# The first layer's gated feed-forward of an audio tower, its fp32 products replaced by three rounded-format products each

## Chip, core and metric

The kernel runs on one core of a Trainium2 chip. The metric is the device time of one execution in microseconds (us), the median of several runs. Five engines work side by side, each through its own instructions in order: TensorE (PE in the rows, its weight loads PEld), VectorE (DVE), ScalarE (ACT), GpSimd (POOL) and SyncE (SP, which issues the DMAs). They wait for each other by semaphores.

## The reference, cut to what matters

The input is (64, 375, 256). A token layer halves the sequence (375 padded to 376, then 188 tokens) with a convolution and a layer norm. Two layers follow; each is an attention and a feed-forward with residuals. The change is in the first layer's feed-forward (width 704), whose operands are quantised to a 4-bit grid with one scale per 16 values:

```
h = tok(x)                                   # conv, mean of two, layer norm with gain and bias
h = h + attn0(layernorm(h))                  # 16 heads over 64 batch entries, softmax
def ffn0(x, w_gate, w_up, w_down):
    xq = fp4_quant_dequant(x)                # blocks of 16 along the last dimension
    g = xq @ fp4_quant_dequant(w_gate).T     # 256 -> 704
    u = xq @ fp4_quant_dequant(w_up).T       # 256 -> 704
    return fp4_quant_dequant(silu(g) * u) @ fp4_quant_dequant(w_down).T   # 704 -> 256
h = h + ffn0(layernorm(h), ...)
h = h + attn1(layernorm(h)); h = h + ffn1(h) # second layer, not touched
```

## The kernel before

**Stages.** `audio_tower` runs `layer0` (token layer and first layer) and then `layer1`. Each has a preparation block, in which weights are loaded and rebuilt, and a main block. All engines end the preparation block before one begins the main block. Between the layers the rows go through a scratch tensor in HBM.

**Preparation of layer0.** DVE quantises the three feed-forward weights, PE transposes them in 44 pieces through two PSUM banks, and ACT copies each piece into `gate_sb`, `up_sb` or `down_sb`.

**Main block of layer0.** The 64 x 188 tokens are worked on in 94 tiles of 128 rows (two token positions of all 64 entries; attention in the first layer runs over the batch entries of one position). The work is a software pipeline: in slot t the tile t goes through the convolution, norms and q, k, v; tile t-1 through scores, softmax and P times V; tile t-2 through the output projection, its norm and the quantisation of xq; tile t-3 through gate, up, tanh and the scales of hh; tile t-4 through hq, down and the store. `slots` unrolls 6 slots ahead of a loop over pairs of slots, and the last ones after it.

The order of each engine within a slot is written out by hand in its `slot` function (from L538 for PE, L616 for ACT, L781 for DVE, L836 for POOL). Nothing is reordered: an instruction that waits holds up all behind it on its engine. In short, for one slot:

- PE: conv, scores, transposes of att, gate and up of columns 0 to 351 (`gateup(t, 0)`), transposes of hq, output projection, `gateup(t, 1)`, `down`, transposes of ln1, transposes of P, q and k, v, P times V, transposes of xq.
- ACT: copy of v, of attT, of h1, tanh 0, exp, copy of hqT (640 and 64 columns), tanh 1, copies of ln1T and PT, magnitude of ln2, copy of q, magnitude of hh, eight copies of k, copy of xqT.
- DVE: division of att, conv result and its statistics, row maximum and shift of the scores, normalisation to h0, first half of hh, h1, statistics of h0 and h1, normalisation to ln1, moments of h1, normalisation to ln2, second half of hh, scales of ln2 and hh, h2, rounding of xq, rounding of hq.
- POOL: scaling of hq, rsqrt 0, h0 times gain, plus bias, rsqrt 1, rsqrt 2, h0b, scaling of hh, scaling of xq. Each rsqrt is an add (L832) and a power (L834) on one column.

**Products.** Gate and up (L468) are fp32: the transposed rows `xqT` (128 x 128, two blocks) are loaded as weights and 352 columns of the weight matrix stream by. Down (L497) takes six blocks of `hqT` and 256 columns of `down_sb`. In the trace an fp32 product is two MATMUL instructions.

**Rounded products.** The second layer already uses `product3` (L867). Each operand is held twice in the rounded format fp32r: a rounded high part, and a low part, which is the value minus the high part. Three matmuls are added up in PSUM: high by low, low by high, high by high.

```
def low(dst, src, hi, done):                 # as in layer1, on DVE there
    dve.tensor_tensor(dst, src, hi.bitcast(fp32), ALU.subtract).then_inc(S[done], 1)
```

Of the kernel before, what the change touches and what calls it, by code (L numbers as in the profile page):

```python
# [167 lines left out]
def layer0(nc, x, conv_w, conv_b, tok_g, tok_b, qkv_w, q_b, k_b, v_b, out_w, out_b, gate_w, up_w, down_w,  # L168
           h2_dram, ident, eps, exponent, w1, w1_loaded, wq, wk, wv, wo):
    with ExitStack() as ctx:  # L170
# [7 lines left out]
        conv_sb = sb("conv_sb", [128, 2 * KC, DM])  # L178
        q_sb, k_sb, v_sb = (sb(n, [128, KC, DM]) for n in ("q_sb", "k_sb", "v_sb"))
        outw_sb = sb("outw_sb", [128, KC, DM])  # L180
        gate_sb, up_sb = sb("gate_sb", [128, KC, F0]), sb("up_sb", [128, KC, F0])
        down_sb = sb("down_sb", [128, len(F0C), DM])
        convb_bc, tokg_bc, tokb_bc, outb_bc = (sb(n, [128, DM]) for n in ("convb_bc", "tokg_bc", "tokb_bc", "outb_bc"))
        qb_col, kb_col, vb_col = (sb(n, [128, KC]) for n in ("qb_col", "kb_col", "vb_col"))
        vb_wide = sb("vb_wide", [128, KC, 128])
# [18 lines left out]
        h1b = [sb(f"h1b{i}", [128, DM]) for i in range(2)]  # L204
        ln2 = sb("ln2", [128, DM])
        xq = sb("xq", [128, DM])
        xqT = sb("xqT", [128, KC, 128])
        tanh_g = sb("tanh_g", [128, GW])
        hh = sb("hh", [128, F0])
        hq = sb("hq", [128, F0])  # L210
        hqT = sb("hqT", [128, len(F0C), 128])
        h2 = [sb(f"h2_{i}", [128, DM]) for i in range(2)]
        binade = sb("binade", [128, 2048])
        small = sb("small", [128, 3, 128])
# [10 lines left out]
        wload, wconst, vones, wfold, vbias = (sem(n) for n in ("wload", "wconst", "vones", "wfold", "vbias"))  # L225
        wgate_loaded, wup_loaded, wdown_loaded = sem("wgate_loaded"), sem("wup_loaded"), sem("wdown_loaded")
        wquant, wtrans, wcopied = sem("wquant"), sem("wtrans"), sem("wcopied")
        with ExitStack() as tmp:
            graw, uraw = (tmp.enter_context(nc.sbuf_tensor(n, [WROWS, F0 // WROWS, DM], fp32)) for n in ("graw", "uraw"))
            draw = tmp.enter_context(nc.sbuf_tensor("draw", [128, KC, F0], fp32))  # L230
            with nc.Block() as block:
                @block.sync
                def _(sp):
# [37 lines left out]
                @block.vector  # L271
                def _(dve):
                    dve.wait_ge(wconst, 6)

                    for v in vblk:
                        for e in range(2):
                            for n in range(2):
                                c = e * (D0 + 1) + D0
                                dve.memset(v[64 * e:64 * e + 64, :, n, c:c + 1], 1.0).then_inc(vones, 1)

                    dve.wait_ge(wload, 16 * 12)
                    dve.wait_ge(wconst, 9)
# [49 lines left out]
                @block.scalar  # L332
                def _(act):
                    for n, (_, dst, rows, cols) in enumerate(JOBS):
                        act.wait_ge(wtrans, n + 1)
                        act.activation(dst, WBANK[n % 2][0:cols, 0:rows], ACT.Copy).then_inc(wcopied, 1)

# [7 lines left out]
            "xq_transposed", "xqT_copied", "gateup_done", "tanh_done", "hh_step", "hqa_step", "hv_ready", "habs_ready", "hqb_step",  # L345
            "hq_ready", "hq_transposed", "hqT_copied", "down_done", "h2_ready", "h2_stored0", "h2_stored1")}

        QK, YS, H1S, ST1, HH, SHIFT, ATT = KC + 4 * KC, 3, 3, 2, 4, 2, 2
        XM = 1 + SCALE_OPS + 1
# [38 lines left out]
        with nc.Block() as block:  # L388
# [25 lines left out]
            def _(pe):  # L414
# [24 lines left out]

                def xq_transpose(t):  # L440
                    bank_free(pe, t, [("ln1T_copied", t, 1, 1)],
                              [("attT_copied", t - 2, 1, 1), ("xqT_copied", t - 3, 1, 1)])
# [15 lines left out]
                def gateup(t, r):  # L458
                    z = t - 3
                    if r == 0:  # L460
                        bank_free(pe, t, [("qk_copied", t - 1, QK, QK), ("vblk_ready", t - 1, 4, 4)],
                                  [("hh_step", t - 4, HH, HH)])
                        wait(pe, "xqT_copied", z + 1)
                    else:
                        wait_step(pe, "hh_step", z, HH, 2)
                    for b, w in ((0, gate_sb), (1, up_sb)):
                        for c in range(KC):
                            last = pe.matmul(gu[:, b, 0:GW], xqT[:, c, :], w[:, c, r * GW:(r + 1) * GW],  # L468
                                             start=c == 0, stop=c == KC - 1)
                    last.then_inc(S["gateup_done"], 1)  # L470

                def att_transpose(t):
                    bank_free(pe, t, [("xqT_copied", t - 3, 1, 1)],
                              [("ln1T_copied", t - 1, 1, 1), ("attT_copied", t - 3, 1, 1)])
                    wait(pe, "att_step", t - 1, ATT)
                    av = att[:].rearrange("p h d -> p (h d)")
                    transposes(tp, [(128 * c, av[:, 128 * c:128 * (c + 1)]) for c in range(KC)], "att_transposed")

                def hq_transpose(t):
                    bank_free(pe, t, [("PT_copied", t - 2, 1, 1)], [("hqT_copied", t - 5, 2, 2)])  # L480
# [11 lines left out]

                def down(t):
                    bank_free(pe, t, [("h1_step", t - 2, H1S, 1)], [("y_step", t, YS, 1), ("h2_ready", t - 5, 1, 1)])
                    wait(pe, "hqT_copied", t - 3, 2)
                    for f, (o, w) in enumerate(F0C):
                        last = pe.matmul(cv[:, 0:DM], hqT[0:w, f, :], down_sb[0:w, f, :], start=f == 0,  # L497
                                         stop=f == len(F0C) - 1)
                    last.then_inc(S["down_done"], 1)

                def ln1_transpose(t):
                    bank_free(pe, t, [("attT_copied", t - 2, 1, 1)],
                              [("xqT_copied", t - 3, 1, 1), ("ln1T_copied", t - 1, 1, 1)])
                    wait(pe, "ln1_ready", t + 1)
                    transposes(tp, [(128 * c, ln1[:, 128 * c:128 * (c + 1)]) for c in range(KC)], "ln1_transposed")

                def p_transpose(t):
                    bank_free(pe, t, [("hqT_copied", t - 4, 2, 2)], [("PT_copied", t - 2, 1, 1)])
                    wait(pe, "probs_ready", t)
                    for i in range(PAIRS):  # L510
                        last = pe.transpose(pt[:, i // 4, 128 * (i % 4):128 * (i % 4 + 1)],
# [53 lines left out]
                        xq_transpose(t)  # L565

                pe.wait_ge(wfold, 6 + 2 * KC)
                pe.wait_ge(wcopied, len(JOBS))
                slots(pe, slot)

            @block.scalar
            def _(act):
# [43 lines left out]
                def slot(t, par):  # L616
# [12 lines left out]
                    if exists(t, 4):  # L629
                        wait(act, "hq_transposed", t - 3)  # L630
                        wait(act, "down_done", t - 4)
                        copy(hqT[:, 0:5, :], pt[:].rearrange("p a b -> p (a b)")[:, 0:640], "hqT_copied")
                        copy(hqT[0:64, 5, :], pt[0:64, 1, 128:256], "hqT_copied")
                    if exists(t, 3):
                        tanh(t - 3, 1)
                    if exists(t, 0):
# [192 lines left out]
            def _(pool):  # L829
                def rsqrt(t, k):  # L830
# [780 lines left out]
```

## Time and profile before

| | |
|---|---|
| median of 3 runs | 5284.75 us (5284.54 to 5287.21) |
| the profiled execution | 5283.22 us, its span 5281.1 us |
| PE busy | 4961.1 us, 94% of the span, 37144 instructions |
| DVE | 3369.7 us, 64% |
| ACT | 2636.0 us, 50% |
| POOL | 1866.8 us, 35% |
| granted TensorE clock, mean | 0.983 of 2.4 GHz |

The profile is of one execution. "Busy" is the union of an engine's instructions, without its waits; the share is of the whole span. The first layer lies from about 74 to 1923 us and the second behind it to the end; they have different limits, so the shares of the whole say little of one stage. In a row of the timeline, "x4" stands for four instructions merged, and the bracket gives the idle time of that engine just before and what ended it.

### The profile page before, as it was taken

The numbers are of one execution on the slowest core, as the hardware profiler recorded it, in microseconds if no ns is written. First come the engines' busy times: TensorE is split into PE (matmuls) and PEld (weight loads), VectorE is DVE, ScalarE is ACT, GpSimd is POOL, SyncE is SP. The second block draws the span as 40 slices with busy tenths as digits, with TensorE's granted clock in tenths as the row PEclk, the third lists the DMA queues.
The fourth block names the chain that finished last, engine by engine and source line by source line (L and its number), as shares of the span: only waits on it lengthen the run. The fifth ranks groups of instructions, "written<-read, shape, count | busy, mean of one in ns | idle before, by whom it ended". The sixth has DMA issues, their size and how long they took to land.

```text
span 5281.1 us, 108766 instructions
## 1 busy us (share of the span) xinstructions
PE 4961.1 (94%) x37144; PEld 4273.4 (81%) x37144; DVE 3369.7 (64%) x7355; ACT 2636.0 (50%) x5824; POOL 1866.8 (35%) x2017
## 2 busy tenths in 40 slices
PE   3999999999999949999999999999999999999997
PEld 2777777777777738998898989989988988989996
DVE  4888888888888843555555555555555555556555
ACT  2555555555555524555545554554554555555553
POOL 1444444444444412323333333333333334233333
PEclk9999999999999979999999999999999999999998
DMA  2000000000000010000000000000000000000000
GB/s 76 19 21 21 19 20 20 21 21 21 21 21 21 19 40 4 7 10 8 10 10 8 7 11 11 7 11 11 7 8 11 10 8 11 10 8 10 10 4 10
DMA packets 64990, 79.53 MB, mean 15 GB/s; under 512 B 8759, under 2 KB 51127, under 8 KB 64439
## 3 DMA queue, kind: packets, MB, share of 16 engines
q1 hardware_dynamic: 64566, 74.07, 4.9%
q8 instruction: 244, 4.00, 0.3%
q14 instruction: 180, 1.47, 0.1%
HBM read 49.40 MB, written 24.64 MB: 14 GB/s over the span
## 4 chain that ended last, share of the span: by engine, by line
PE 61%; issue 1%; DVE 1%; POOL 0%; ACT 0%; DMA 0%; SPq 0%; DVEq 0%; ACTq 0%; POOLq 0%
PE bA L869 10%; PE bA L870 8%; PE bA L871 8%; PE bO L1166 5%; PE bS L1145 4%; PE bO L1169 3%; PE bO L1172 3%; PE bA L1223 2%; PE bB L869 2%; PE bS L1146 2%; PE bS L1149 2%; PE bB L1136 2%; PE bB L1135 2%; PE bB L870 2%; PE bB L871 2%; PE bA L1224 2%
## 5 line engine op out<-in xcount | busy, mean ns | idle before, releaser
L1528 POOL TENSOR_TENSOR sqs_lo<-sq,sqs_hi 128x768 fp32r<-128x768 f32 x256 | 477.8, 1866 | 1065.7 <-ACT sqs_hi L1276 1058.4
L1370 DVE TENSOR_TENSOR qk_lo<-bA,qk_hi 128x384 fp32r<-128x384 f32 x512 | 284.4, 556 | 608.1 <-ACT qk_hi L1276 596.3
L1297 ACT ACTIVATE phiq<-bB 64x384 f32<-64x384 f32 x512 | 248.8, 486 | 792.5 <-PE bB L1136 786.2
L1520 POOL TENSOR_TENSOR yT_lo<-tanh_y,yT_hi 128x384 fp32r<-128x384 f32 x256 | 259.1, 1012 | 622.2 <-ACT yT_hi L1276 622.0
L1380 DVE TENSOR_TENSOR aT<-bS,mask 128x768 f32<-128x768 f32 x256 | 245.2, 958 | 158.7 <-PE bS L1149 158.7
L1166 PE MATMUL bO<-V,aT 128*128 128x65 f32 x2048 | 310.9, 274 | 0.0
L1145 PE MATMUL bS<-phiq,phik 128*128 128x256 f32 x1024 | 304.8, 379 | 0.0
L1328 ACT ACTIVATE pre<-bA,fc1b,fc1s 128x384 f32<-128x384 f32 x256 | 171.8, 671 | 251.3 <-PE bA L1224 251.3
L1166 PEld LDWEIGHTS bO<-V,aT 128*128 128x128 f32 x2048 | 275.3, 190 | 17.6 <-issue 0.2
L468 PE MATMUL gu<-gate_sb,xqT 128*128 128x352 f32 x752 | 266.9, 478 | 22.2 <-DVE hh L721 20.6
L1276 ACT ACTIVATE qk_hi<-bA 128x384 fp32r<-128x384 f32 x512 | 250.2, 489 | 64.0 <-PE bA L871 57.9
L497 PE MATMUL bank<-down_sb,hqT 128*128 128x256 f32 x1128 | 279.1, 389 | 1.0 <-ACT hqT L574 1.0
L1285 ACT ACTIVATE sq<-bA 128x384 f32<-128x384 f32 x512 | 251.5, 491 | 52.7 <-DVE qk_lo L1370 46.9
L614 ACT ACTIVATE tanh_g<-gu 128x352 f32<-128x352 f32 x188 | 87.3, 464 | 381.6 <-PE gu L468 381.6
L590 ACT ACTIVATE kblk<-gu,kb_masked,rowmask 128x128 f32<-128x128 f32 x752 | 271.5, 465 | 0.0
L109 POOL TENSOR_TENSOR hh<-hh,small 128x704 f32<-128x704 f32 x94 | 135.1, 1438 | 375.2 <-DVE small L103 375.2
L497 PEld LDWEIGHTS bank<-down_sb,hqT 128*128 128x128 f32 x1128 | 207.6, 190 | 72.3 <-issue 32.7
L468 PE MATMUL gu<-up_sb,xqT 128*128 128x352 f32 x752 | 255.7, 463 | 0.0
L869 PE MATMUL bA<-fc_lo,yT_hi 128*128 128x256 f32 x768 | 230.3, 300 | 10.7 <-POOL yT_lo L1520 5.6
L869 PE MATMUL bB<-qk_lo,omega_hi 128*128 128x384 f32 x512 | 186.4, 364 | 48.0 <-issue 42.9
L869 PE MATMUL bA<-wv_lo,xT_hi 128*128 128x256 f32 x768 | 228.6, 298 | 1.0 <-ACT sq L1285 1.0
L869 PE MATMUL bA<-wo_lo,attT_hi 128*128 128x256 f32 x768 | 225.9, 294 | 1.1 <-ACT pre L1328 1.1
(234 smaller groups left out, 15403.7 us busy)
## 6 DMA issues: line engine op xcount, KB each, us to landing
xT<-in_x SPq DMA_DIRECT2D x94, 256.0 KB, 2.7
h_scratch<-h SPq DMA_DIRECT2D x188, 64.0 KB, 1.9
hx<-h_scratch SPq DMA_DIRECT2D x32, 256.0 KB, 2.8
out<-res SPq DMA_DIRECT2D x32, 256.0 KB, 2.2
hx<-h_scratch SPq DMA_DIRECT2D x64, 64.0 KB, 2.5
out<-res SPq DMA_DIRECT2D x64, 60.0 KB, 1.8
q<-in_fc_q SPq DMA_DIRECT2D x2, 1024.0 KB, 6.2
wq_sb<-in_wq SPq DMA_DIRECT2D x1, 1024.0 KB, 5.0
```

Source lines behind the costliest of these rows:

```text
L468: last = pe.matmul(gu[:, b, 0:GW], xqT[:, c, :], w[:, c, r * GW:(r + 1) * GW], start=c == 0, stop=c == KC - 1)
L497: last = pe.matmul(cv[:, 0:DM], hqT[0:w, f, :], down_sb[0:w, f, :], start=f == 0, stop=f == len(F0C) - 1)
L590: act.activation(kblk[:, c, :, j, :], src, ACT.Identity, bias=kb_masked[:, c, j:j + 1], scale=rowmask[:, j:j + 1]).then_inc(S["qk_copied"], 1)
L869: pe.matmul(out, lhs[0], rhs[1], start=start, stop=False)
L870: pe.matmul(out, lhs[1], rhs[0], start=False, stop=False)
L871: return pe.matmul(out, lhs[0], rhs[0], start=False, stop=stop)
L1145: pe.matmul(o[:, :, 0:HEAD], keys, phiq[b][:, :, HEAD * i:HEAD * (i + 1)], start=True, stop=True)
L1166: pe.matmul(O[:, dst(i)], aT0[b][:, i, h, 0:HEAD], V[:, i, v], start=True, stop=True)
L1285: act.activation(sq[:, i, :], A[:, i, 0:NT], ACT.Square).then_inc(S["qk_hi"], 1)
L1370: dve.tensor_tensor(dst, src, hi.bitcast(fp32), ALU.subtract).then_inc(S[done], 1)
L1520: pool.tensor_tensor(yT[1][:, f % RING, :], tanh_y[f % 2][:], yT[0][:, f % RING, :].bitcast(fp32), ALU.subtract).then_inc(S["y_lo"], 1)
L1528: pool.tensor_tensor(sqs[1][:], sq[:], sqs[0][:].bitcast(fp32), ALU.subtract).then_inc(S["sq_lo"], 1)
```

## The change

The feed-forward weights are held as `gate_hi`, `gate_lo`, `up_hi`, `up_lo`, `down_hi`, `down_lo`; the full ones live in the preparation only. At its end ACT makes four rounded copies and DVE four subtractions. In the main block ACT copies each of xqT and hqT twice from PSUM, rounded and full, POOL subtracts one from the other, and gate, up and down are `product3`. New semaphores `xqT_split` and `hqT_split` say that the low parts are there; counts of the copies are doubled where PSUM banks are waited for.

```
# preparation
+ dve.wait_ge(whigh, n + 1)                                # four times: gate, up, down (5 blocks), down (last)
+ dve.tensor_tensor(lo, full, hi.bitcast(fp32), ALU.subtract).then_inc(wlow, 1)
+ act.wait_ge(wcopied, len(JOBS))
+ for hi, full in ((gate_hi, gate_sb), (up_hi, up_sb)):
+     act.activation(hi[:], full[:], ACT.Copy).then_inc(whigh, 1)
+ act.activation(down_hi[:, 0:5, :], down_sb[:, 0:5, :], ACT.Copy).then_inc(whigh, 1)
+ act.activation(down_hi[0:64, 5, :], down_sb[0:64, 5, :], ACT.Copy).then_inc(whigh, 1)
# PE, gateup
-         wait(pe, "xqT_copied", z + 1)
+         wait(pe, "xqT_split", z + 1)
-             last = pe.matmul(gu[:, b, 0:GW], xqT[:, c, :], w[:, c, r * GW:(r + 1) * GW], ...)
+             last = product3(pe, gu[:, b, 0:GW], (xqT_hi[:, c, :], xqT_lo[:, c, :]),
+                             (hi[:, c, cols], lo[:, c, cols]), c == 0, c == KC - 1)
# PE, down
-     wait(pe, "hqT_copied", t - 3, 2)
+     wait(pe, "hqT_split", t - 3, 2)
-         last = pe.matmul(cv[:, 0:DM], hqT[0:w, f, :], down_sb[0:w, f, :], ...)
+         last = product3(pe, cv[:, 0:DM], (hqT_hi[0:w, f, :], hqT_lo[0:w, f, :]),
+                         (down_hi[0:w, f, :], down_lo[0:w, f, :]), f == 0, f == len(F0C) - 1)
# PE, waits for banks: ("xqT_copied", t - 3, 1, 1) -> (.., 2, 2) and ("hqT_copied", .., 2, 2) -> (.., 4, 4)
# ACT, slot
      wait(act, "down_done", t - 4)
-     copy(hqT[:, 0:5, :], pt...[:, 0:640], "hqT_copied")
-     copy(hqT[0:64, 5, :], pt[0:64, 1, 128:256], "hqT_copied")
+     wait(act, "hqT_split", t - 4, 2)
+     for dst in (hqT_hi, hqT):
+         copy(dst[:, 0:5, :], pt...[:, 0:640], "hqT_copied")
+         copy(dst[0:64, 5, :], pt[0:64, 1, 128:256], "hqT_copied")
...
      wait(act, "gateup_done", t - 2, 2)
+     wait(act, "xqT_split", t - 2)
+     copy(xqT_hi[:], tp[:, 0:256], "xqT_copied")
      copy(xqT[:], tp[:, 0:256], "xqT_copied")
# POOL, slot
+ def low(dst, src, hi, done):
+     pool.tensor_tensor(dst, src, hi.bitcast(fp32), ALU.subtract).then_inc(S[done], 1)
          wait(pool, "st1", t + 1, ST1)
          rsqrt(t, 1)
+     if exists(t, 4):
+         wait(pool, "hqT_copied", t - 3, 4)
+         low(hqT_lo[:, 0:5, :], hqT[:, 0:5, :], hqT_hi[:, 0:5, :], "hqT_split")
+         low(hqT_lo[0:64, 5, :], hqT[0:64, 5, :], hqT_hi[0:64, 5, :], "hqT_split")
      if exists(t, 2):
          wait(pool, "h1_step", t - 1, H1S)
          rsqrt(t - 2, 2)
...
          fp4_scaled(pool, xq[:], xq[:], small_x, 1, 128, DM).then_inc(S["xq_ready"], 1)
+     if exists(t, 2):
+         wait(pool, "xqT_copied", t - 1, 2)
+         low(xqT_lo[:], xqT[:], xqT_hi[:], "xqT_split")
```

## Rows read from the trace of the kernel before

**Rows 1.** Busy time by stretch: us, each engine's busy time (instructions), PE clock, DMA.

```profile
1000.00:1500.00 500.00, 473.30 (x3704) 358.41 (x3700) 410.44 (x867) 271.38 (x692) 205.55 (x315) 1.00 0.08 21
```

**Rows 2.** One tile's instructions, 500 to 1500 us: ns min/median/max, first and last start.

```profile
L574 ACT ACTIVATE PT_sb<-pt x53: 1024/1024/1025, 503.0 to 1491.5; 128x1024 f32<-128x1024 f32 x53
```

**Rows 3.** Timeline of one slot: start, length, engine, line, operation, [idle before, releaser].

```profile
1003.51 0.42 ACT L574 ACTIVATE xqT<-bank 128x256 f32<-128x256 f32 x1
...
1005.23 1.35 PE L468 MATMUL gu<-gate_sb,xqT 128*128 128x352 f32 x4
...
1006.47 0.19 POOL L832 TENSOR_TENSOR rstd<-moments,eps 128x1 f32<-128x1 f32 x1 [1.85 <-DVE moments L672]
...
1007.60 0.82 PE L483 MATMUL pt<-ident,hq 128*128 128x128 f32 x6
...
1008.85 0.73 POOL L846 TENSOR_TENSOR h<-h,tokb_bc 128x256 f32<-128x256 f32 x1
...
1009.18 0.85 ACT L574 ACTIVATE hqT<-pt 128x640 f32<-128x640 f32 x2
...
1009.70 0.41 DVE L802 BATCH_NORM_STATS2 stats<-h 128x6 f32<-128x256 f32 x1
...
1010.80 0.55 POOL L834 TENSOR_TENSOR rstd<-rstd,exponent 128x1 f32<-128x1 f32 x1
1011.46 0.41 DVE L676 TENSOR_SCALAR ln<-h,moments,rstd 128x256 f32<-128x256 f32 x1 [0.65 <-POOL rstd L834]
...
1011.79 0.17 DVE L672 BATCH_NORM_AGGREGATE moments<-stats 128x2 f32<-128x6 f32 x1
1011.98 2.95 PE L497 MATMUL bank<-down_sb,hqT 128*128 128x256 f32 x12
1012.04 0.19 POOL L832 TENSOR_TENSOR rstd<-moments,eps 128x1 f32<-128x1 f32 x1 [0.69 <-DVE moments L672]
...
1012.90 0.81 DVE L676 TENSOR_SCALAR ln<-h,moments,rstd 128x256 f32<-128x256 f32 x1 [0.94 <-POOL rstd L834]
...
1014.85 0.44 PE L418 MATMUL bank<-ident,ln 128*128 128x128 f32 x2
...
1017.46 1.44 POOL L109 TENSOR_TENSOR hh<-hh,small 128x704 f32<-128x704 f32 x1 [3.90 <-DVE small L103]
...
1018.13 1.04 DVE L127 SCALAR_TENSOR_TENSOR ln<-binade_x,ln 128x256 f32<-128x256 f32 x1 [0.15 <-ACT binade_x L577]
...
1020.48 0.41 PE L418 MATMUL bank<-ident,xq 128*128 128x128 f32 x2 [0.55 <-POOL xq L109]
```

**Rows 4.** Groups of POOL's instructions in the second layer, 2400 to 5200 us.

```profile
L1528 POOL TENSOR_TENSOR sqs_lo<-sq,sqs_hi 128x768 fp32r<-128x768 f32 x219 | 409.5, 1870 | 862.9 <-ACT sqs_hi L1276 856.2
L1520 POOL TENSOR_TENSOR yT_lo<-tanh_y,yT_hi 128x384 fp32r<-128x384 f32 x221 | 223.8, 1013 | 517.3 <-ACT yT_hi L1276 517.1
```

**Rows 5.** Timeline of PE in the second layer: rounded products, 256 and 384 columns.

```profile
3003.48 0.28 PE L871 MATMUL bA<-wv_hi,xT_hi 128*128 128x256 f32 x1
...
3005.24 0.28 PE L871 MATMUL bA<-wv_hi,xT_hi 128*128 128x256 f32 x1
...
3011.35 0.34 PE L870 MATMUL bA<-xT_hi,wq_lo 128*128 128x384 f32 x1
...
3013.12 0.34 PE L871 MATMUL bA<-xT_hi,wk_hi 128*128 128x384 f32 x1
```

**Rows 6.** Busy time by stretch where PE had waited.

```profile
144.50:148.50 4.00, 2.30 (x21) 1.81 (x17) 3.78 (x6) 3.69 (x11) 1.43 (x3) 1.00 0.00 0
1974.70:1978.70 4.00, 1.32 (x9) 1.20 (x8) 0.42 (x1) 0.81 (x2) 1.80 (x1) 1.00 0.00 0
1979.00:1982.00 3.00, 3.00 (x11) 3.00 (x11) 0.00 (x0) 1.55 (x4) 0.00 (x0) 0.50 0.00 0
```

**Rows 7.** Timeline of the second layer's preparation: weight copy and subtraction.

```profile
1925.39 1.91 ACT L951 ACTIVATE wq_hi<-wq_sb 128x2048 fp32r<-128x2048 f32 x1 [8.70 <-PEq L388]
...
1939.61 2.29 DVE L967 TENSOR_TENSOR wq_lo<-wq_sb,wq_hi 128x2048 fp32r<-128x2048 f32 x1
```

More of the change, by code:

```diff
@@ L180, in layer0 @@
         outw_sb = sb("outw_sb", [128, KC, DM])
-        gate_sb, up_sb = sb("gate_sb", [128, KC, F0]), sb("up_sb", [128, KC, F0])
-        down_sb = sb("down_sb", [128, len(F0C), DM])
+        gate_hi, up_hi = sb("gate_hi", [128, KC, F0], fp32r), sb("up_hi", [128, KC, F0], fp32r)
+        gate_lo, up_lo = sb("gate_lo", [128, KC, F0], fp32r), sb("up_lo", [128, KC, F0], fp32r)
+        down_hi, down_lo = (sb(n, [128, len(F0C), DM], fp32r) for n in ("down_hi", "down_lo"))
         convb_bc, tokg_bc, tokb_bc, outb_bc = (sb(n, [128, DM]) for n in ("convb_bc", "tokg_bc", "tokb_bc", "outb_bc"))
@@ L206, in layer0 @@
         xq = sb("xq", [128, DM])
-        xqT = sb("xqT", [128, KC, 128])
+        xqT, xqT_hi, xqT_lo = (sb(n, [128, KC, 128], t) for n, t in (("xqT", fp32), ("xqT_hi", fp32r), ("xqT_lo", fp32r)))
         tanh_g = sb("tanh_g", [128, GW])
@@ L210, in layer0 @@
         hq = sb("hq", [128, F0])
-        hqT = sb("hqT", [128, len(F0C), 128])
+        hqT, hqT_hi, hqT_lo = (sb(n, [128, len(F0C), 128], t) for n, t in
+                               (("hqT", fp32), ("hqT_hi", fp32r), ("hqT_lo", fp32r)))
         h2 = [sb(f"h2_{i}", [128, DM]) for i in range(2)]
@@ L227, in layer0 @@
         wquant, wtrans, wcopied = sem("wquant"), sem("wtrans"), sem("wcopied")
+        whigh, wlow = sem("whigh"), sem("wlow")
         with ExitStack() as tmp:
@@ L230, in layer0 @@
             draw = tmp.enter_context(nc.sbuf_tensor("draw", [128, KC, F0], fp32))
+            gate_sb, up_sb, down_sb = (tmp.enter_context(nc.sbuf_tensor(n, s, fp32)) for n, s in (
+                ("gate_sb", [128, KC, F0]), ("up_sb", [128, KC, F0]), ("down_sb", [128, len(F0C), DM])))
             with nc.Block() as block:
@@ L306, in _ @@
                     st.end()
+                    for n, (lo, full, hi) in enumerate((
+                            (gate_lo[:], gate_sb[:], gate_hi[:]), (up_lo[:], up_sb[:], up_hi[:]),
+                            (down_lo[:, 0:5, :], down_sb[:, 0:5, :], down_hi[:, 0:5, :]),
+                            (down_lo[0:64, 5, :], down_sb[0:64, 5, :], down_hi[0:64, 5, :]))):
+                        dve.wait_ge(whigh, n + 1)
+                        dve.tensor_tensor(lo, full, hi.bitcast(fp32), ALU.subtract).then_inc(wlow, 1)
                 JOBS = [(raw, j, c, WROWS, 128, dst, c, j * WROWS) for raw, dst in ((graw, gate_sb), (uraw, up_sb))
@@ L344, in layer0 @@
             "att_transposed", "attT_copied", "outproj_done", "h1_step", "h1b_ready", "xq_step", "xabs_ready", "xq_ready",
-            "xq_transposed", "xqT_copied", "gateup_done", "tanh_done", "hh_step", "hqa_step", "hv_ready", "habs_ready", "hqb_step",
-            "hq_ready", "hq_transposed", "hqT_copied", "down_done", "h2_ready", "h2_stored0", "h2_stored1")}
+            "xq_transposed", "xqT_copied", "xqT_split", "gateup_done", "tanh_done", "hh_step", "hqa_step", "hv_ready", "habs_ready", "hqb_step",
+            "hq_ready", "hq_transposed", "hqT_copied", "hqT_split", "down_done", "h2_ready", "h2_stored0", "h2_stored1")}
         QK, YS, H1S, ST1, HH, SHIFT, ATT = KC + 4 * KC, 3, 3, 2, 4, 2, 2
@@ L441, in xq_transpose @@
                     bank_free(pe, t, [("ln1T_copied", t, 1, 1)],
-                              [("attT_copied", t - 2, 1, 1), ("xqT_copied", t - 3, 1, 1)])
+                              [("attT_copied", t - 2, 1, 1), ("xqT_copied", t - 3, 2, 2)])
                     wait(pe, "xq_ready", t - 1)
@@ L462, in gateup @@
                                   [("hh_step", t - 4, HH, HH)])
-                        wait(pe, "xqT_copied", z + 1)
+                        wait(pe, "xqT_split", z + 1)
                     else:
                         wait_step(pe, "hh_step", z, HH, 2)
-                    for b, w in ((0, gate_sb), (1, up_sb)):
+                    cols = slice(r * GW, (r + 1) * GW)
+                    for b, hi, lo in ((0, gate_hi, gate_lo), (1, up_hi, up_lo)):
                         for c in range(KC):
-                            last = pe.matmul(gu[:, b, 0:GW], xqT[:, c, :], w[:, c, r * GW:(r + 1) * GW],
-                                             start=c == 0, stop=c == KC - 1)
+                            last = product3(pe, gu[:, b, 0:GW], (xqT_hi[:, c, :], xqT_lo[:, c, :]),
+                                            (hi[:, c, cols], lo[:, c, cols]), c == 0, c == KC - 1)
                     last.then_inc(S["gateup_done"], 1)
                 def att_transpose(t):
-                    bank_free(pe, t, [("xqT_copied", t - 3, 1, 1)],
+                    bank_free(pe, t, [("xqT_copied", t - 3, 2, 2)],
                               [("ln1T_copied", t - 1, 1, 1), ("attT_copied", t - 3, 1, 1)])
@@ L479, in hq_transpose @@
                 def hq_transpose(t):
-                    bank_free(pe, t, [("PT_copied", t - 2, 1, 1)], [("hqT_copied", t - 5, 2, 2)])
+                    bank_free(pe, t, [("PT_copied", t - 2, 1, 1)], [("hqT_copied", t - 5, 4, 4)])
                     wait(pe, "hq_ready", t - 3)
@@ L494, in down @@
                     bank_free(pe, t, [("h1_step", t - 2, H1S, 1)], [("y_step", t, YS, 1), ("h2_ready", t - 5, 1, 1)])
-                    wait(pe, "hqT_copied", t - 3, 2)
+                    wait(pe, "hqT_split", t - 3, 2)
                     for f, (o, w) in enumerate(F0C):
-                        last = pe.matmul(cv[:, 0:DM], hqT[0:w, f, :], down_sb[0:w, f, :], start=f == 0,
-                                         stop=f == len(F0C) - 1)
+                        last = product3(pe, cv[:, 0:DM], (hqT_hi[0:w, f, :], hqT_lo[0:w, f, :]),
+                                        (down_hi[0:w, f, :], down_lo[0:w, f, :]), f == 0,
+                                        f == len(F0C) - 1)
                     last.then_inc(S["down_done"], 1)
@@ L502, in ln1_transpose @@
                     bank_free(pe, t, [("attT_copied", t - 2, 1, 1)],
-                              [("xqT_copied", t - 3, 1, 1), ("ln1T_copied", t - 1, 1, 1)])
+                              [("xqT_copied", t - 3, 2, 2), ("ln1T_copied", t - 1, 1, 1)])
                     wait(pe, "ln1_ready", t + 1)
@@ L507, in p_transpose @@
                 def p_transpose(t):
-                    bank_free(pe, t, [("hqT_copied", t - 4, 2, 2)], [("PT_copied", t - 2, 1, 1)])
+                    bank_free(pe, t, [("hqT_copied", t - 4, 4, 4)], [("PT_copied", t - 2, 1, 1)])
                     wait(pe, "probs_ready", t)
@@ L567, in _ @@
                 pe.wait_ge(wfold, 6 + 2 * KC)
-                pe.wait_ge(wcopied, len(JOBS))
+                pe.wait_ge(wlow, 4)
                 slots(pe, slot)
@@ L631, in slot @@
                         wait(act, "down_done", t - 4)
-                        copy(hqT[:, 0:5, :], pt[:].rearrange("p a b -> p (a b)")[:, 0:640], "hqT_copied")
-                        copy(hqT[0:64, 5, :], pt[0:64, 1, 128:256], "hqT_copied")
+                        wait(act, "hqT_split", t - 4, 2)
+                        for dst in (hqT_hi, hqT):
+                            copy(dst[:, 0:5, :], pt[:].rearrange("p a b -> p (a b)")[:, 0:640], "hqT_copied")
+                            copy(dst[0:64, 5, :], pt[0:64, 1, 128:256], "hqT_copied")
                     if exists(t, 3):
```

## Prediction

> **What bounds the kernel now.** I read the stretches first. In the first layer's steady part TensorE (PE) is busy 473.3 of 500 us at full clock [rows 1]: it looks like the bound, 94.7%. One slot (one of 94 tiles) takes (1491.5 - 503.0) / 52 = 19.01 us [rows 2], so PE works 18.0 us of it and waits 1.0. Then I read one slot in order of time and followed what ends PE's waits [rows 3]. Its last piece, the transposes of xq, waits 0.55 us for GpSimd (POOL), which got xq from VectorE (DVE). Going back from there, a chain closes on itself: PE conv and scores, DVE's row maximum and shift, its normalisation, POOL's two products for h0 (the second ends at 1009.58), DVE's statistics of h0 (1009.70), POOL's rsqrt 1 (ends 1011.35), DVE's normalisation of ln1 (1011.46) and moments of h1 (end 1011.96), POOL's rsqrt 2 (starts 1012.04), DVE's normalisation of ln2 (1012.90). From there DVE works on with one gap, of 0.15 us (1018.13), up to xq; POOL scales xq, PE transposes it (1020.48), and the next conv follows. So the period is that of this DVE/POOL chain. Of PE only the xq transposes, conv and scores are in it. Gate, up and down, which the change touches, lie beside it.
>
> **PE work removed.** An fp32 product is two instructions, a rounded one is one. Now: four gate products and four instructions of up of a half (1005.23 to 1007.60, [rows 3]) are 8 instructions in 2.37 us, 0.296 us each, so 0.59 us a product. Rounded products in the second layer: 15 instructions of 256 columns from 3003.48 to 3005.24 are 0.117 us each; 10 of 384 columns from 3011.35 to 3013.12 are 0.177 [rows 5]. For 352 columns I interpolate 0.162. A half becomes 12 x 0.162 = 1.94 us, 0.43 less; the second half the same. Down is 12 instructions in 2.87 us (1011.98 to 1014.85) and becomes 18 x 0.117 = 2.11, 0.76 less. PE does 0.43 + 0.43 + 0.76 = 1.6 us less a slot.
>
> What the chain gets of it: the first half ends 0.43 earlier, so tanh and the first DVE products of hh do too; but the statistics of h0 then wait for POOL's product that ends at 1009.58, so they start at about 1009.64 instead of 1009.70. Gain 0.06 us. rsqrt 1 ends at 1011.29.
>
> **The split of xq** (ACT one copy more, POOL one subtraction of 256). ACT copies xqT at 1003.51 in 0.42 us; with a second copy behind it both are done by 4.35 (times from here on are us after 1000, in this slot). POOL subtracts 256 elements. Two rows of POOL subtractions with rounded output give 1013 ns for 384 and 1870 ns for 768 [rows 4], that is 0.156 + 2.23 ns an element: 0.73 us, to 5.1. Behind it in POOL's queue stands the scaling of hq, 1.4 us (as the 128x704 scaling at 1017.46), so to 6.5, when DVE's work beside it is in PSUM; then rsqrt 0, issued at 6.47 before. The gate products started at 5.23, and the transposes of hq, which wait for the scaling, at 7.60 (7.2 now). Everything meets its time with up to 0.7 us to spare or none: I cost it at nothing. If ACT were 0.2 us later, rsqrt 0 would be late by about that, and the normalisation to h0 and the chain with it by no more than that: 0.2.
>
> **The split of hq** (ACT two copies more, POOL two subtractions, 640 and 64 elements). Both copies now take 0.85 us from 9.18 [rows 3]; ACT starts no later and does four, to 10.9 at most. POOL is in rsqrt 1 until 11.29 and, in program order, the two subtractions stand right after it and ahead of rsqrt 2. By the same two rows they cost 0.156 + 2.23 x 640 = 1.58 and 0.156 + 2.23 x 64 = 0.30, together 1.88 [rows 4]: POOL is free at 13.17. But DVE's normalisation of ln1 and the moments of h1 also stand before rsqrt 2. What DVE does beside a POOL instruction: the product of 256 at 1018.13 took 1.04 us and ended 0.27 us after POOL's scaling of hh (17.46 + 1.44 = 18.90) [rows 3], as if it only streamed once POOL was done. ln1's normalisation starts at 11.40, in the first subtraction (11.29 to 12.87), so it ends shortly after that, at about 13.0; the moments of h1, 0.17, are done when POOL is free. rsqrt 2 starts at about 13.25, where it started at 12.04: +1.2 us, with the gain of 0.06 already taken off. The Trainium skill, SBUF — State Buffer, section "SBUF: two separate sides", calls the port pair of VectorE and GpSimd an exclusive lock held for the whole instruction, the loser fully blocked; that row agrees (0.27 us after POOL's end). If the two shared the ports instead, ln1 would be done well before POOL is free, and the delay would be 13.17 - 12.04 = 1.13; the lock may add up to 0.3.
>
> Bounds: subtractions as cheap as POOL's scaling of hh (1.44 us for 704, [rows 3]; 1.57 for the two after a fixed part each) instead of 1.88: free at 12.86, +0.8 us. Above, with ln1 held back by both subtractions: 13.17 + 0.15 for its rest + 0.17 for the moments is 13.5, +1.45. I take 1.2 because the rows that give 1.88 are the same operation with the same output format.
>
> All that follows rsqrt 2 in the chain (h0b, ln2, the second half of hh, scales, xq, hq) is as now and has no slack: xq comes 1.2 us later, so do the next conv and scores. New period about 20.2 us.
>
> **The wait of down.** Down could start 0.86 earlier than its 11.98, at 11.1, and waits for the low part until 13.2: 2.1 us idle. Queued behind: ln1's transposes, P's, q, k, v, PV, xq's. From ln1's transposes (14.85) to the end of PV (20.48 less the 0.55 of waiting) PE takes 5.1 us. With down 2.1 long it ends PV at 13.2 + 2.1 + 5.1 = 20.4; xq's transposes are due at 20.48 + 1.2 = 21.7: hidden, with 1.2 us to spare, as long as the clock stays. The other new waits (ACT for the subtractions of the slot before, PE's bank waits for twice the count) are met a slot earlier.
>
> **Once.** The weight splits stand after the last weight copy and before the barrier; after it the loop's first loads start, and the first conv waits for them. ACT copies at 1.91 us for 2048 elements and DVE subtracts at 2.29 [rows 7]; first copy 1408: 1.33; then DVE 1.6, 1.6, 1.45, 0.4: together 6.4 us. DVE is nearly back to back, ACT's later copies are beside it. In the last slots nothing covers copies and subtraction ahead of the last down: +2.6, less about 1 for shorter down at low clock: +2.
>
> **Sum.** 92 slots x 1.2 = 110; + 6.4 + 2 = 118.4. The profiled execution took 5283.2 (span 5281.1 and 2.1 around it), 1.5 below the median of the runs. So 5401.6 in its terms, 5403 in the median's.
>
> **Rivals.**
> 1. *The clock falls.* Nothing in the steady part loses it now. It stayed at full after PE was busy 2.30 of 4 us; it fell to half (1.2 GHz) after 1.32 of 4, and stood at half for the next 3 us shown [rows 6]. The new gap leaves 1.9 of 4: between. 3 us at half cost PE 1.5, of which 1.2 are covered: +0.3 a slot where it happens, more where it stays longer. In every slot +28, at twice that price +55. Beside the 5403: 5410 to 5458. The Trainium skill, TensorE: Matmul & The Clock Gate, section "What's actually happening", says that the throttled state is the default and activity lifts it; the two rows agree in kind. By that rule alone the time would be this rival's. Chance 0.2.
> 2. *PE sets the period* (other side: faster). PE is busy 94.7% [rows 1]; if every us taken off PE shortened the slot, 1.6 x 94 = 150 less, 8 more for what comes once: 5143. It needs rsqrt 2 not to be delayed, so the subtractions would have to fit in the 0.69 us between rsqrt 1 and rsqrt 2. At 1.57 at least they don't. It decides from a delay of rsqrt 2 under 0.06 us, the gain found above. Against it: PE waits for xq at the end of the slot [rows 3], so PE is not the one that is late. For it: its share. 0.08.
> 3. *The subtractions are cheap*, as POOL's scalings are, so that rsqrt 2 is 0.8 to 0.9 late: 92 x 0.8 + 8.4 + 5284.7 = 5367, to 5376. Against it: both subtraction rows. 0.09.
> 4. Delay and gains cancel within measurement: 0.03; no mechanism in the rows gives it.
>
> **How the numbers follow.** Forecast 0.60, its own range 5376 to 5427 (0.9 to 1.45 us a slot). Rival 1 0.20, rival 3 0.09, rival 2 0.08, rival 4 0.03. The range to hold 8 in 10 goes from 5355 (rival 3 in) to 5450 (rival 1 in) and leaves out rivals 2 and 4 and tails. A change of over 0.2% (10.6 us) can be told from none: slower 0.89, same 0.03, faster 0.08.
>
> **What would show it.** The period between two copies of PT in the first layer: 20.2 us, PE busy 16.4 of it. rsqrt 2's POOL add 1.9 us after rsqrt 1's end instead of 0.69, released by DVE's moments or by POOL itself. Subtractions of 640 at 1.5 to 1.6 us. PE idle about 2 us before down, ended by POOL, and about 1 us before xq's transposes. ln1's normalisation near 1.5 us instead of 0.41. Granted clock 1.00 in the steady part. The first conv 6.4 us later. The second layer unchanged. I am wrong if rsqrt 2 is not later, if the period is under 19.5 (rival 2), or if the clock in the steady part is under 0.97 (rival 1).

## The result and the profile after

The changed kernel takes 5432.9 us (median of 4 runs, 5431.7 to 5433.3), the one before 5284.7: ratio 1.028, 95% interval 1.026 to 1.030. It is slower by 148 us. The profiled execution has a span of 5431.5 us.

First the same two views as [rows 1] and [rows 2]: busy time in 1000 to 1500 us, and the copies of PT in 500 to 1500 us.

```profile
1000.00:1500.00 500.00, 428.32 (x3730) 373.08 (x3729) 397.51 (x806) 271.68 (x703) 256.09 (x369) 0.96 0.07 19
```

```profile
L592 ACT ACTIVATE PT_sb<-pt x49: 1023/1024/1026, 499.6 to 1481.2; 128x1024 f32<-128x1024 f32 x49
```

The slot is (1481.2 - 499.6) / 48 = 20.45 us, 1.44 more than before. PE is busy 85.7% instead of 94.7%, and the granted clock is 0.96 instead of 1.00. Over the whole first layer the copies of PT run from 105.9 to 1871.9 before and from 112.7 to 2013.3 after: 134.6 us in the slots and 6.8 at the start; the layer's end adds 1.6. Of the 150.4 us between the spans, 143.0 lie in the first layer (up to the second layer's first weight copy, which starts at 1925.4 before and at 2068.4 after) and 7.4 in the second, whose code is the same.

One slot in order of time, as in [rows 3] (start, length, engine, line, operation, [idle before, releaser]):

```profile
1001.38 0.74 POOL L871 TENSOR_TENSOR h<-h,tokb_bc 128x256 f32<-128x256 f32 x1
...
1002.16 0.43 DVE L824 BATCH_NORM_STATS2 stats<-h 128x6 f32<-128x256 f32 x1 [0.29 <-POOL h L871]
...
1003.27 0.55 POOL L856 TENSOR_TENSOR rstd<-rstd,exponent 128x1 f32<-128x1 f32 x1
...
1003.79 1.99 POOL L859 TENSOR_TENSOR hqT_lo<-hqT,hqT_hi 128x640 fp32r<-128x640 f32 x2
...
1003.93 1.54 DVE L698 TENSOR_SCALAR ln<-h,moments,rstd 128x256 f32<-128x256 f32 x1 [0.65 <-POOL rstd L856]
1005.39 0.17 DVE L694 BATCH_NORM_AGGREGATE moments<-stats 128x2 f32<-128x6 f32 x1
1005.75 0.18 POOL L854 TENSOR_TENSOR rstd<-moments,eps 128x1 f32<-128x1 f32 x1
...
1005.93 0.37 PE L901 MATMUL bank<-down_lo,hqT_hi 128*128 128x256 f32 x1 [2.14 <-POOL hqT_lo L859]
...
1006.59 0.81 DVE L698 TENSOR_SCALAR ln<-h,moments,rstd 128x256 f32<-128x256 f32 x1 [1.03 <-POOL rstd L856]
...
1009.91 0.44 PE L434 MATMUL bank<-ident,ln 128*128 128x128 f32 x2
...
1012.62 0.43 DVE L127 SCALAR_TENSOR_TENSOR ln<-binade_x,ln 128x256 f32<-128x256 f32 x1 [0.94 <-ACT binade_x L595]
```

Rsqrt 1 ends at 1003.82 and rsqrt 2 starts at 1005.75: 1.93 us apart, where they were 0.69 apart [rows 3]. The two subtractions fill that gap. DVE's normalisation of ln1 takes 1.54 us instead of 0.41 and ends at 1005.47, 0.15 after the first subtraction. PE waits 2.14 us for the low part ahead of down.

Then down takes from 1005.93 to 1009.91, 3.98 us, where 2.1 was forecast. The busy time by stretch around it (columns as in [rows 1]):

```profile
1002.00:1006.00 4.00, 1.86 (x13) 1.60 (x11) 2.60 (x5) 1.32 (x4) 2.97 (x6) 1.00 0.00 0
1006.20:1009.50 3.30, 3.30 (x16) 3.08 (x15) 2.77 (x8) 0.00 (x0) 1.05 (x2) 0.50 0.00 0
```

After 4 us with 1.86 us of work the clock fell to 1.2 GHz for the whole of down. This does not happen in every slot. Three slots later the clock stayed at full after nearly the same stretch (its busy time, then that of down; below it PE's rows of the same slot):

```profile
1063.78:1067.78 4.00, 1.93 (x13) 1.67 (x12) 2.73 (x6) 1.47 (x5) 3.03 (x6) 1.00 0.00 0
1068.00:1070.00 2.00, 2.00 (x17) 1.87 (x17) 1.53 (x3) 0.00 (x0) 1.11 (x2) 1.00 0.00 0
```

```profile
1067.78 0.36 PE L901 MATMUL bank<-down_lo,hqT_hi 128*128 128x256 f32 x1 [2.07 <-POOL hqT_lo L859]
...
1070.26 0.44 PE L434 MATMUL bank<-ident,ln 128*128 128x128 f32 x2
...
1076.03 0.41 PE L434 MATMUL bank<-ident,xq 128*128 128x128 f32 x2 [0.69 <-POOL xq L109]
```

Here down takes 2.48 us (1067.78 to 1070.26), and PE later waits 0.69 us for xq. In the slot whose clock fell that wait is gone: PE's transposes of xq start at 1014.92 without one.

```profile
1014.92 0.44 PE L434 MATMUL bank<-ident,xq 128*128 128x128 f32 x2
```

So a fall makes down 1.5 us longer (3.98 instead of 2.48), the wait of 0.7 covers that much of it, and PE is in the chain for the rest, 0.8.

What decides which slots fall is not shown: the wait ahead of down was 2.04 to 2.14 us in the slots that fell and 2.07 to 2.10 in the others. The exp of ACT, once a slot, shows them (start and length, copied from 500 to 600 us):

```profile
509.61 1.05 ACT L646 ACTIVATE P<-P 128x1024 f32<-128x1024 f32 x1
529.78 1.05 ACT L646 ACTIVATE P<-P 128x1024 f32<-128x1024 f32 x1
549.72 1.05 ACT L646 ACTIVATE P<-P 128x1024 f32<-128x1024 f32 x1
570.63 1.05 ACT L646 ACTIVATE P<-P 128x1024 f32<-128x1024 f32 x1
591.47 1.05 ACT L646 ACTIVATE P<-P 128x1024 f32<-128x1024 f32 x1
```

Slots of 20.17 and 19.94 us alternate with slots of 20.91 and 20.84. The short pair averages 20.06, 1.05 above the 19.01 of before; the long ones cost 0.8 more, and about half of the slots are long. So the slot's 1.44 us are 1.05 from a delay in every slot and 0.39 from the clock.

### The profile page after: what moved, and what is told of

Read it like the earlier page. It is cut to its first block, busy times and chain, and to the rows that moved or that the text cites. A ratio compares the mean times of both kernels' runs of the same rounds, so it can differ in the third digit from the quotient of the medians.

```text
span 5431.5 us, 112180 instructions
## 1 busy us (share of the span) xinstructions
PE 4926.0 (91%) x38460; PEld 4437.6 (82%) x38460; DVE 3435.4 (63%) x7359; ACT 2727.1 (50%) x6110; POOL 2111.3 (39%) x2299
## 4 chain that ended last, share of the span: by engine, by line
PE 59%; issue 1%; DVE 0%; ACT 0%; POOL 0%; DMA 0%; SPq 0%; DVEq 0%; ACTq 0%; POOLq 0%
PE bA L901 10%; PE bA L902 8%; PE bA L903 8%; PE bO L1198 5%; PE bS L1177 4%; PE bO L1201 3%; PE bO L1204 2%; PE bA L1255 2%; PE bB L901 2%; PE bS L1178 2%; PE bS L1181 2%; PE bB L1168 2%; PE bB L1167 2%; PE bB L903 2%; PE bB L902 2%; PE bA L1256 2%
## 5 line engine op out<-in xcount | busy, mean ns | idle before, releaser
L901 PE MATMUL bank<-down_lo,hqT_hi 128*128 128x256 f32 x564 | 209.0, 371 | 194.8 <-POOL hqT_lo L859 194.8
L901 PEld LDWEIGHTS bank<-down_lo,hqT_hi 128*128 128x128 f32 x564 | 136.5, 242 | 235.4 <-DVE moments L694 211.4
L698 DVE TENSOR_SCALAR ln<-h,moments,rstd 128x256 f32<-128x256 f32 x188 | 217.1, 1155 | 161.3 <-POOL rstd L856 161.3
L592 ACT ACTIVATE ln1T<-bank 128x256 f32<-128x256 f32 x94 | 36.1, 384 | 497.5 <-PE bank L434 497.5
L1402 DVE TENSOR_TENSOR attT_lo<-bT,attT_hi 128x384 fp32r<-128x384 f32 x256 | 142.6, 557 | 129.3 <-ACT attT_hi L1308 129.1
```

Source lines behind the costliest of these rows:

```text
L901: pe.matmul(out, lhs[0], rhs[1], start=start, stop=False)
```

## The experiments

All are compared with the kernel before in the same job. "Slot" is the mean period between two exps of ACT from 500 to 1500 us.

| run | median us | ratio (95%) | slot us | steady clock |
|---|---|---|---|---|
| before | 5285 | 1 | 19.01 | 1.00 |
| changed | 5432.9 | 1.028 (1.026 to 1.030) | 20.46 | 0.96 |
| e1 gate and up only | 5282.5 | 0.9997 (0.9988 to 1.0007) | 18.91 | 1.00 |
| e2 down only | 5404.4 | 1.022 (1.021 to 1.024) | 20.26 | 1.00 |
| e3 filler | 5396.6 | 1.021 (1.019 to 1.022) | 20.11 | 1.00 |
| e4 no wait | 5428.7 | 1.027 (1.025 to 1.029) | 20.48 | 0.98 |
| e5 short low | 5289.2 | 1.0014 (1.0005 to 1.0023) | 18.96 | 1.00 |
| e6 low behind h0b | 5736.8 | 1.086 (1.084 to 1.088) | 23.89 | 0.86 |
| e7 h0b early, on before | 5246.9 | 0.994 (0.993 to 0.995) | 18.62 | 1.00 |
| e8 e1 with h0b early | 5242.3 | 0.992 (0.991 to 0.994) | 18.47 | 1.00 |
| e9 changed with h0b early | 5430.4 | 1.028 (1.026 to 1.029) | 20.48 | 0.95 |
| e10 extra behind rsqrt 2 | 5412.9 | 1.024 (1.023 to 1.026) | 20.48 | 0.97 |
| e11 extra ahead of rsqrt 2 | 5420.7 | 1.026 (1.024 to 1.027) | 20.48 | 0.98 |
| e12 e9 with filler | 5359.8 | 1.014 (1.013 to 1.016) | 19.70 | 1.00 |

**Half of the change each (e1, e2).**

```
e1  - product3 in down, its splits (ACT copies, POOL subtractions, weights); down reads hqT, down_sb in fp32
e2  - product3 in gateup and its splits; gate and up read xqT, gate_sb, up_sb in fp32
```

> Gate and up rounded, down fp32 as before the change. Theory (the subtractions of hq ahead of rsqrt 2 on POOL are the loss, and PE is not in the chain): without them the slot is 19.01 - 0.06 us, the weight split costs about 5 us once: 5279 to 5290 us, clock 1.00 in the steady part. Rival (PE sets the period and only the wait of down spoiled it): 0.86 us a slot less, 5210 us. Rival (the split of xq is also on the path): over 5300 us.

> Down rounded, gate and up fp32. Theory: rsqrt 2 is as late as in the changed kernel, period 20.1 us; PE's idle before down is 0.86 us shorter (about 1.3 us), so the clock should stay at full: 5385 to 5400 us. If the clock falls as often as in the changed kernel: 5433. If the split of xq carried a part of the loss: well under 5385.

Gate and up alone change nothing that can be measured in the total: the slot is 0.1 us shorter, the weights' split comes once. So 0.86 us of PE work a slot is worth almost nothing, and no cost of the split of xq shows. PE did not set the period. Down alone brings the loss without the clock: 20.26 us, PE's wait before down is 1.34 us (the view of e2's PE), and the clock stays at 1.00.

```profile
1011.66 0.39 PE L891 MATMUL bank<-down_lo,hqT_hi 128*128 128x256 f32 x1 [1.34 <-POOL hqT_lo L852]
```

The 5404 is above the forecast 5385 to 5400. The slot is 0.15 us longer than the 20.11 of e3 below, which has gate and up rounded too; that is about the gain of e1's usual slots.

**The clock (e3).**

```
  def down(t): ...
+     for f in range(12):
+         pe.matmul(cv[:, 0:DM], xqT_hi[:, f % KC, :], gate_hi[:, f % KC, 0:DM], start=True, stop=True)
      wait(pe, "hqT_split", t - 3, 2)
```

> The changed kernel with 12 more products of 256 columns (about 1.4 us) ahead of PE's wait for the low part of hq; their result is overwritten. Theory (1.07 us a slot from POOL's queue, 0.37 from the clock): PE idle 0.7 us instead of 2.1, the clock stays at full, 5395 to 5405 us. Rival (the clock costs nothing, PE has slack): 5433 us. Rival (PE sets the period): slower than 5433, up to 5565.

With useless products in the gap the kernel is 36 us faster than the changed one, as forecast. Every slot is 19.97 to 20.26 us, as long as the slots of the changed kernel whose clock stayed at full (19.93 to 20.23). This is the delay alone.

**PE's wait alone (e4).**

```
- wait(pe, "hqT_split", t - 3, 2)
+ wait(pe, "hqT_copied", t - 3, 4)
+ wait(pe, "hqT_split", t - 4, 2)         # low part of the slot before, from the other of two buffers
```

> The low part of hq in two buffers; down reads that of the slot before, so PE does not wait for the subtraction, and POOL does all its work in the same places. The output is not the reference's (down uses the low part of another tile). Theory: POOL's delay of rsqrt 2 stays, the clock is at full: 20.1 us a slot, 5395 to 5405 us. Rival (PE's wait for down is the loss): back to 5290 us or less.

The time stayed near the changed kernel's: neither theory's number. Most slots are as forecast, 19.99 and 20.26 us; every fourth takes 21.7. These are rows of exp across one such slot, the stretches in it, and conv in it and in the next:

```profile
1038.47 1.05 ACT L648 ACTIVATE P<-P 128x1024 f32<-128x1024 f32 x1
1060.12 1.05 ACT L648 ACTIVATE P<-P 128x1024 f32<-128x1024 f32 x1
1080.10 1.05 ACT L648 ACTIVATE P<-P 128x1024 f32<-128x1024 f32 x1
```

```profile
1048.00:1052.00 4.00, 2.65 (x54) 2.41 (x53) 3.59 (x9) 2.13 (x6) 1.86 (x2) 1.00 0.10 24
1053.00:1055.00 2.00, 2.00 (x5) 1.65 (x6) 1.47 (x3) 2.00 (x8) 0.00 (x1) 0.50 0.28 91
```

```profile
1052.92 3.40 PE L452 MATMUL bank<-conv_sb,xT 128*128 128x256 f32 x8
...
1074.17 1.89 PE L452 MATMUL bank<-conv_sb,xT 128*128 128x256 f32 x8
```

PE's idle time only moved: 1.70 us ahead of the transposes of xq and 1.14 ahead of those with q_sb, instead of 2.14 ahead of down. There the clock fell too, with PE busy 2.65 of the 4 us before, and there the slowed product is conv, which is in the chain (3.40 us here; 1.89 in the next slot, at full clock). So such a fall costs 1.4 us (21.67 instead of 20.26) and not 0.8. The wait of down by itself is not the loss, but removing it doesn't save the clock.

**The length of the subtraction (e5).**

```
- low(hqT_lo[:, 0:5, :], hqT[:, 0:5, :], hqT_hi[:, 0:5, :], "hqT_split")
+ low(hqT_lo[:, 0, 0:64], hqT[:, 0, 0:64], hqT_hi[:, 0, 0:64], "hqT_split")
```

> The changed kernel with the first subtraction of hq cut from 640 to 64 columns (the rest of the low part is zero, so down is less exact). Theory (the length of the subtraction delays rsqrt 2): POOL is busy 0.3 + 0.5 us between rsqrt 1 and rsqrt 2 instead of 2.0; rsqrt 2 is 0.1 to 0.3 us later than before the change, PE idle before down about 1 us, clock full: 5300 to 5320 us. Rival (PE's waits and the number of instructions matter, not their length): above 5390.

The same instructions and waits, the first subtraction with a tenth of the columns (about 0.3 us instead of 1.53): the slot is 18.96 us, no longer than before the change, and the clock does not fall. The 5289 is below the forecast 5300 to 5320: between rsqrt 1 and rsqrt 2 lie 0.79 us, only 0.1 more than before, less than the gain of the earlier gate (e5's POOL):

```profile
1014.52 0.55 POOL L858 TENSOR_TENSOR rstd<-rstd,exponent 128x1 f32<-128x1 f32 x1
1015.03 0.86 POOL L861 TENSOR_TENSOR hqT_lo<-hqT,hqT_hi 128x64 fp32r<-128x64 f32 x2
1015.86 0.18 POOL L856 TENSOR_TENSOR rstd<-moments,eps 128x1 f32<-128x1 f32 x1
```

**Another place for it (e6).**

```
  rsqrt(t - 2, 2); ...; h0b
+ low(hqT_lo ...), low(hqT_lo ...)        # moved here from ahead of rsqrt 2
```

> The changed kernel with the subtractions of hq moved behind rsqrt 2 and h0b. Theory: rsqrt 2 is on time again, but down waits until about 15.6 (of the slot in the rows) instead of 13.2, and PE becomes the chain: 15.6 + 2.1 + 5.1 = 22.8 against 20.5, 2.3 us a slot: 5500 us at full clock; with the clock at half after a 4.5 us gap in every slot up to 1.7 us more, 5660. Rival (only the delay of rsqrt 2 counts, PE has room): back to 5290.

Now PE waits 4.28 us for the low part and becomes the chain, at a steady clock of 0.86: 23.9 us a slot. The kernel is slower than the forecast allowed (5737 against 5660 at most). The forecast had 21.3 us a slot at full clock and up to 1.7 for the clock; down alone took 4.41 us in this slot (1026.95 to 1031.36), 2.3 more than its 2.1. Subtracting later is no cure.

```profile
1026.95 0.55 PE L901 MATMUL bank<-down_lo,hqT_hi 128*128 128x256 f32 x1 [4.28 <-POOL hqT_lo L859]
...
1031.36 0.69 PE L434 MATMUL bank<-ident,ln 128*128 128x128 f32 x2
```

**Only POOL's instruction, nothing waiting for it (e11, e10).** On the kernel before, with fp32 products:

```
+ pool.tensor_tensor(idle_c[:], idle_a[:], idle_b[:], ALU.subtract)   # 128x640, own tiles; e11: ahead of rsqrt 2, e10: behind it
```

> The kernel before with the same subtraction between rsqrt 1 and rsqrt 2; nothing waits for it, and PE's products are as before. Theory (the POOL queue alone carries the main part of the loss): rsqrt 2 is late by 1.53 - 0.69 + blocking of ln1 = 0.9 to 1.1 us, clock full: 5370 to 5390 us. Rival (the loss needs PE's wait for down): 5285 us.

> The kernel before with one more POOL subtraction of 128x640 on tiles of its own, behind rsqrt 2 and ahead of h0b; nothing waits for it. Theory (a POOL instruction that runs first blocks DVE's normalisation of ln2 until it ends): 1.5 us a slot for it, less the 0.4 that h0b blocked, if h0b then runs beside unblocked work: 0.8 to 1.2 us a slot, 5360 to 5400 us. Rival (the two engines share the ports, nothing is blocked): 5285 to 5310 us.

In e11 three slots of four are 20.09 to 20.2 us, 1.1 above before: POOL's queue alone gives the delay. The fourth is 21.55 us: there the clock fell during conv. In e10 the slots at full clock are 19.77 to 19.88 us, 0.8 more; three of eight are 21.5. Both runs came out above the forecast, which had a full clock. With every slot at full clock, 92 slots of 20.12 and of 19.82 us would give 5388 and 5360 (an estimate from these rows), inside both forecasts. Its POOL and DVE:

```profile
1017.06 1.53 POOL L859 TENSOR_TENSOR idle_c<-idle_a,idle_b 128x640 f32<-128x640 f32 x1
1017.13 1.61 DVE L681 TENSOR_SCALAR ln<-h,moments,rstd 128x256 f32<-128x256 f32 x1 [0.93 <-POOL rstd L839]
```

DVE's 0.41 us operation began 0.07 us after POOL's and ended 0.15 us after it. The Trainium skill, SBUF — State Buffer, section "SBUF: two separate sides", has this as an exclusive lock for a whole instruction; these rows agree with it (1.61 us instead of 0.41), and they do not agree with shared ports.

**The block that was there before (e7, e8, e9, e12).** In [rows 3] ln2's normalisation takes 0.81 us (1012.90 to 1013.71), and h0b runs beside it on the kernel before:

```profile
1012.83 0.73 POOL L855 TENSOR_TENSOR h0b<-h,outb_bc 128x256 f32<-128x256 f32 x1
```

```
          pool.tensor_tensor(h0[:], h0[:], tokb_bc[:], ALU.add)
+         pool.tensor_tensor(h0b[par][:], h0[:], outb_bc[:], ALU.add)   # moved from behind rsqrt 2
          rsqrt(t, 1)
```

> The kernel before, with h0b moved ahead of rsqrt 1 on POOL, where POOL was idle 0.96 us. Theory (the DVE/POOL chain sets the period, and ln2's normalisation is blocked 0.4 us by h0b on POOL): 0.3 to 0.4 us less a slot, 5247 to 5257 us. Rival (PE at 94.7% sets the period, or the block is hidden): 5285 us.

> Gate and up rounded, down fp32, and h0b ahead of rsqrt 1. Theory: as the run with h0b alone, plus some 5 us for the weight split, less 0.06 us a slot, and less again if PE had begun to bound there: 5235 to 5257 us. Rival (PE bound): 5210 or less.

> The changed kernel with h0b ahead of rsqrt 1, as in the run on the kernel before, where it took 0.39 us off the slot. Theory (the chain ln2 to xq sets the period here too): about 0.4 us a slot off the slots at full clock, and the clock falls about as often: 5390 to 5405 us. Rival (where the clock falls PE has taken over and h0b gives nothing): 5410 to 5420 us.

> The changed kernel with both h0b ahead of rsqrt 1 and the 12 filler products. Theory (the two terms add up: 37 us for the clock, 37 for h0b): 5355 to 5365 us. If they overlap: 5390 us.

e7's slot is 0.39 us shorter. ln2's normalisation takes 0.41 us:

```profile
1011.95 0.55 POOL L834 TENSOR_TENSOR rstd<-rstd,exponent 128x1 f32<-128x1 f32 x1
1012.53 0.41 DVE L676 TENSOR_SCALAR ln<-h,moments,rstd 128x256 f32<-128x256 f32 x1 [0.93 <-POOL rstd L834]
```

e8 is the fastest kernel here, 41 us below before; the intervals of e7 and e8 overlap. On the changed kernel the same move gives nothing (e9, 5430.4, above the range of the theory and that of the rival): the slots at full clock are 0.4 us shorter, 19.53 and 19.78, but two of three are now long, 20.9. The long ones are no shorter than those of the changed kernel: there PE is in the chain, as the rival had it, and the clock falls more often besides. What the chain gained, the clock took. With the filler as well (e12) the two terms add up: 5359.8, in the middle of the forecast.

## Why the prediction was right, and where it was off

The side and the main cause were right, and the range of 5355 to 5450 holds the 5432.9. The likeliest case does not: it had 5403, with a range of its own of 5376 to 5427. What happened is that case together with rival 1 (5410 to 5458, chance 0.2), and the steady clock of 0.96 is the sign that the prediction had named for being wrong (under 0.97). The range held because it was drawn wide enough to take rival 1 in. By its steps:

- *PE is not in the chain.* Right while the clock is full (it waits 0.7 us for xq there), not in the slots in which it falls. e1 takes 0.86 us of PE work out of the slot for 0.1 us. This ends rival 2 (faster, 5143).
- *The chain's gain, 0.06 us.* Too small: e1's slots are mostly 18.97 and 18.72, on average 0.17 shorter (two of the 52 took 20.6; the clock fell in them, after PE was busy 2.44 of 4 us in the one at 941 us). I had read one slot of the loop's two. In it the statistics of h0 wait for POOL; in the other they wait for DVE's own hh and h1, which end after POOL's product, and the earlier gate gives 0.25. These are the rows of that other slot before the change:

```profile
1027.84 0.73 POOL L846 TENSOR_TENSOR h<-h,tokb_bc 128x256 f32<-128x256 f32 x1
...
1028.53 0.42 DVE L735 TENSOR_TENSOR h<-bank,h0b 128x256 f32<-128x256 f32 x1
1028.87 0.42 DVE L802 BATCH_NORM_STATS2 stats<-h 128x6 f32<-128x256 f32 x1
```

- *Subtractions of 1.58 and 0.30 us.* 1.53 and 0.50; together 1.99 with 1.88 forecast. Rival 3 (cheap subtractions) is out.
- *Rsqrt 2 late by 1.2 us.* 1.93 - 0.69 = 1.24 after rsqrt 1, less the gain of 0.17: 1.07, measured 1.05 in the slots at full clock and 1.10 in e3. e11 shows the delay with nothing else of the change, e5 shows it gone with the length.
- *ln1's normalisation blocked.* Right, 1.54 us. The moments are done at 1005.56, before POOL is free, so the block itself costs nothing on top.
- *Down's wait is hidden, with the clock at full.* The wait was 2.14 us, as forecast. "The clock stays" is the step that failed: it was given 0.6 against 0.2 for its fall. It fell in about half of the slots, for 36 us in all (e3). With it the sum is 5403 - 12 for the smaller delay + 36 = 5427; the 6 left are about what the second layer adds. I compared the 4 us ahead of a fall by their busy time; e4 fell after 2.65 us of 4, more than the 2.30 after which [rows 6] show it at full, and the changed kernel stayed at full after 1.93. So those rows gave no safe side.
- *The price of a fall, 0.3 us (rival 1).* The 1.5 us lost by PE is right; "1.2 are covered" is not. Down takes 2.48 us at full clock where 2.1 was forecast, and PE has 0.7 us to spare ahead of xq's transposes instead of 1.2. So a fall costs 0.8. That it came in half of the slots only makes 0.39 on average, inside the 0.3 to 0.6 of the rival: that agreement is luck.
- *Once.* At the start 6.8 where 6.4 was forecast; at the end 1.6 where 2 was.
- *The second layer unchanged.* Its code is, but it took 3363.1 us from its first weight copy instead of 3355.7. In the other profiles this part is between 3354.0 and 3364.5: 3355.6 in e7, 3363.4 in e8, and 3354.0 in e5, which has the rounded products too. Single executions of the kernel before lie as far apart (5274.8 to 5290.1 over all runs). No run was made on it; the cause stays open.

## What to carry to other kernels

Find the queue that is in the chain and count what a new instruction delays behind it: 2.0 us of subtraction in a 0.7 us pause of POOL held rsqrt 2 back by 1.24 us, and each slot by 1.05, while 0.86 us of matmul time saved beside the chain returned 0.17 (e1). An engine that gets less to do, or waits longer, can also lose its clock, and then a saving elsewhere is taken back (e9). Moving one POOL operation into a real pause, away from a DVE operation that it blocks, was worth more here (36 us, e7) than the faster product format.

## What the runs showed of the hardware that was not expected

- The clock fell in e11, whose PE was busy 90% of the steady part (below, columns as in [rows 1]), and whose only long wait in a slot was 1.7 us. The cost depends on what runs then: 0.8 us where it was down, 1.4 to 1.6 where it was mainly conv.

```profile
1000.00:1500.00 500.00, 449.43 (x3442) 339.78 (x3440) 408.87 (x808) 249.78 (x634) 226.87 (x316) 0.98 0.07 19
```

The waits of PE in the same stretch (who waited for whom: us in all, times, longest):

```profile
PE bank L423 <- POOL xq L109: 42.1, 25, 1.7
PE gu L473 <- DVE hh L726: 5.4, 24, 0.2
```

- Useless products in a wait made the changed kernel 36 us faster than leaving PE idle (e3), and 71 us with h0b early (e9 to e12).
- The second subtraction took 0.50 us where 0.30 was forecast. It has 128 columns on 64 partitions, and I had counted 64 columns: POOL's time went by the columns. By the forecast's own line, 128 columns come to 0.44. In e5 the subtraction of 64 columns on all 128 partitions took 0.32, less than this one.
